# Loading a block's token rows in two transfers of 64 rows, each left out where it holds no row of the block

## The reference, cut to what matters

```
logits = x @ router_w.T + expert_bias
probs = sigmoid(logits); top_w, top_idx = top_k(probs, 8)
h1 = silu(einsum('th,eih->eti', x, w_gate))          # 256 -> 128 per expert
routed = einsum('eti,ehi->th', h1 * combine, w_down) # 128 -> 256, summed over 8 experts
x = layernorm(x + routed + shared)
```

## Time and profile before

| what | value |
|---|---|
| median of the three runs | 1122.46 us |
| profiled execution, its own time | 1123.29 us |
| its span, first to last instruction | 1121.5 us |
| mean granted TensorE clock | 0.951 |
| busy share of the span: TensorE, VectorE, ScalarE, GpSimd | 85%, 76%, 56%, 67% |
| DMA in the expert stage: busy share of the 16 engines | about 0.9 |

### The profile page before, as it was taken

How to read it: one execution, slowest core, us unless ns; L and a number is a source line. 1 busy time by engine, 2 the same in 40 slices (tenths; PEclk the granted TensorE clock), 3 DMA queues, 4 the chain that set the end, 5 groups by cost and what they waited for, 6 DMA issues and landing times. The chain is left out here.

```text
span 1121.5 us, 17555 instructions
## 1 busy us (share of the span) xinstructions
PE 957.9 (85%) x4878; PEld 801.3 (71%) x4878; DVE 848.6 (76%) x1645; ACT 625.9 (56%) x1555; POOL 746.0 (67%) x648
## 2 busy tenths in 40 slices
PE   6598989999999999999987989706989999899475
PEld 4476767888887887887866877605878778787354
DVE  0669999899999999999999994764656555555175
ACT  4766685875874865865864644403545555545100
POOL 1445576748679888888978986564777777777400
PEclk9698999999999999999988999957999999999699
DMA  7472854924124224134133012238998989997596
GB/s 237 169 253 77 252 171 151 300 71 162 45 63 143 76 68 153 62 100 133 40 126 118 37 48 75 101 120 260 326 301 262 297 281 287 285 294 244 187 377 222
DMA packets 118461, 195.48 MB, mean 174 GB/s; under 512 B 17684, under 2 KB 83378, under 8 KB 115922
## 3 DMA queue, kind: packets, MB, share of 16 engines
q1 hardware_dynamic: 79890, 134.54, 37.5%
q0 software_dynamic: 16512, 35.19, 8.6%
q10 hardware_dynamic: 21952, 24.51, 6.8%
HBM read 155.21 MB, written 75.64 MB: 206 GB/s over the span
## 5 line engine op out<-in xcount | busy, mean ns | idle before, releaser
L449 POOL TENSOR_TENSOR inf_all<-bc_all,du 128x1024 f32<-128x1024 f32 x128 | 300.6, 2365 | 102.3 <-DVEq L1647 62.0
L1649 DVE TENSOR_TENSOR_SCAN DA<-DA,inf_all 128x1024 f32<-128x1024 f32 x128 | 293.1, 2289 | 15.8 <-ACT DA L712 12.9
L1104 PE MATMUL Y<-hb_all,ident 128*128 128x256 f32 x1024 | 248.6, 391 | 21.9 <-DVE u L1665 21.6
L2196 POOL DMA_INDIRECT yp_dram<-u,sz x216 | 212.8, 985 | 78.9 <-issue 45.7
L1104 PEld LDWEIGHTS Y<-hb_all,ident 128*128 128x128 f32 x1024 | 197.6, 196 | 55.4 <-DVE u L1665 26.1
L712 ACT ACTIVATE DA<-dl,a_neg 128x255 f32<-128x255 f32 x512 | 211.9, 461 | 0.2
L2263 ACT ACTIVATE u<-DA,sz 128x256 f32<-128x256 f32 x216 | 102.3, 474 | 117.3 <-DMA yp_dram<-u,sz 83.7
L1656 DVE TENSOR_TENSOR hb_all<-DA,bc_all 128x1024 f32<-128x1024 f32 x128 | 156.0, 1219 | 7.9 <-DVE DA L1649 0.5
L2231 PE MATMUL DA<-hb_all,sz 128*128 128x256 f32 x432 | 136.5, 398 | 20.1 <-ACT sz L2256 19.0
L2224 PE MATMUL DA<-sz,hb_all 128*128 128x128 f32 x864 | 133.2, 277 | 3.8 <-issue 3.8
L2224 PEld LDWEIGHTS DA<-sz,hb_all 128*128 128x128 f32 x864 | 114.7, 193 | 4.2 <-issue 4.2
(11 more groups left out here) (453 smaller groups left out, 1599.9 us busy)
## 6 DMA issues: line engine op xcount, KB each, us to landing
hb_all<-in_w_moe SPq DMA_DIRECT2D x216, 256.0 KB
bc_all<-bc_dram SPq DMA_DIRECT2D x32, 1024.0 KB, 5.8
inf_all<-xe_dram SPq DMA_DIRECT2D x216, 140.0 KB
bc_all<-yp_dram SPq DMA_DIRECT2D x16, 1024.0 KB, 6.1
xe_dram<-zeros ACTq DMA_DIRECT2D x2, 7420.0 KB, 25.7
xe_dram<-zeros ACTq DMA_DIRECT2D x1, 7560.0 KB, 26.9
yp_dram<-u,sz POOLq DMA_INDIRECT x216
xt<-in_xT SPq DMA_DIRECT2D x8, 256.0 KB, 6.0
```

Of the source, the lines that this page charges most:

```text
L449: g.tensor_tensor(inf[(b * NTAU + t) % NI][:, :, :], bc[gr][:, 0, :, :], du[p][:, c, :].unsqueeze(1).to_broadcast([P, SG, T]), ALU.mult).t ...
L1104: ins = mm(Y[:, 0:T], ident[:, :], hb[t % NH][:, n, :], start=gr == 0 and n == 0, stop=gr == NG - 1 and n == SG - 1, skip_group_check=True)
L1649: v.tensor_tensor_scan(da[:, :], da[:, :], inf[(b * NTAU + t) % NI][:, :, :].rearrange("p n t -> p (n t)"), 0.0, ALU.mult, ALU.add).then_i ...
L2196: g.indirect_dma_start(yp_dram, bass.IndirectOffsetOnAxis(ap=pid[:, half * UNROLL + s_:half * UNROLL + s_ + 1], axis=0), ys[s_][:, :], Non ...
```

## The change

A block's rows are loaded by two transfers of 64 rows (`PARTS` = 2). The table has three values for a block (two row offsets and the weights' offset). VectorE adds a large number to the offset of a part in which no row belongs to the block, from turn 1 on; a transfer with such an offset is left out, as the weights' already are, and its semaphore still counts. In turn 0 both parts of all blocks are loaded. `ways` now takes the values of two blocks (6) in one load. Who waited for 16 on a slot's semaphore now waits for 32.

```diff
+SKIPPED = 1 << 19
+PARTS = 2
+PROWS = P // PARTS
+PWAY = PARTS + 1
...
-        xg_in = [sig(f"xg_in{i}", 16) for i in range(UNROLL)]
+        xg_in = [sig(f"xg_in{i}", 16 * PARTS) for i in range(UNROLL)]
...
-            def ways(i, h):
+            def ways(i, s_):
                 _, got = nc.values_load_multi_w_load_instructions(
-                    tabs[0:1, bass.ds((i * UNROLL + h * QUAD) * 2, QUAD * 2)], engines=[mybir.EngineType.SP],
+                    tabs[0:1, bass.ds((i * UNROLL + s_) * PWAY, PAIR * PWAY)], engines=[mybir.EngineType.SP],
...
-            def tokens(i, s_, r):
+            def tokens(i, s_, parts):
                 if gt_d.at(i - 1, s_ // PAIR + 1, True):
                     sp.wait_ge(gt_d.sem, gt_d.at(i - 1, s_ // PAIR + 1))
-                sp.dma_start(xg_i[s_].bitcast(U8), rows_at[bass.ds(r, P * X_BYTES)].rearrange("(p c) -> p c", p=P)).then_inc(xg_in[s_].sem, 16)
+                for f, r in enumerate(parts):
+                    sp.dma_start(xg_i[s_][f * PROWS:(f + 1) * PROWS, :].bitcast(U8),
+                                 rows_at[bass.ds(r, PROWS * X_BYTES)].rearrange("(p c) -> p c", p=PROWS),
+                                 bounds_check="skip_entire_dma").then_inc(xg_in[s_].sem, 16)
...
             def body(i):
-                for h in range(UNROLL // QUAD):
-                    got = ways(i, h)
-                    for q in range(QUAD):
-                        tokens(i, h * QUAD + q, got[q][0])
-                        weights(i, h * QUAD + q, got[q][1])
+                for lo in range(0, UNROLL, PAIR):
+                    for q, (parts, w) in enumerate(ways(i, lo)):
+                        tokens(i, lo + q, parts)
+                        weights(i, lo + q, w)
...
-                pe.wait_ge(xg_in[s_].sem, xg_in[s_].at(i, 16))
+                pe.wait_ge(xg_in[s_].sem, xg_in[s_].at(i, 16 * PARTS))
...
+            v.scalar_tensor_tensor(first_row[:, :], blk_b[:, :], float(P), blk_s[:, :], ALU.mult, ALU.subtract)
+            v.scalar_tensor_tensor(end_row[:, :], blk_q[:, :], float(P), blk_s[:, :], ALU.add, ALU.subtract)
+            v.tensor_scalar(later[:, :], turn_f[:, :], 0.0, None, ALU.is_gt)
...
-            v.tensor_scalar(way[:, :, 0], blk_h[:, :], float(X_BYTES), None, ALU.mult)
+            for f in range(PARTS):
+                v.tensor_scalar(missed[:, :, f], first_row[:, :], float((f + 1) * PROWS), None, ALU.is_ge)
+                ins = v.tensor_scalar(part_at[:, :, f], blk_h[:, :], float(f * PROWS), None, ALU.add)
+            link(ins)
+            for f in range(PARTS):
+                ins = v.scalar_tensor_tensor(missed[:, :, f], end_row[:, :], float(f * PROWS), missed[:, :, f], ALU.is_le, ALU.max)
+            link(ins)
+            link(v.scalar_tensor_tensor(missed[:, :, :], missed[:, :, :], float(SKIPPED),
+                                        later[:, :].unsqueeze(2).to_broadcast([BJ, 3, PARTS]), ALU.mult, ALU.mult))
+            link(v.tensor_tensor(part_at[:, :, :], part_at[:, :, :], missed[:, :, :], ALU.add))
+            v.tensor_scalar(way[:, :, 0:PARTS], part_at[:, :, :], float(X_BYTES), None, ALU.mult)
```

More of the change, by code:

```diff
@@ L98, in decoder_kernel @@
         blk_dram = nc.dram_tensor("blk_dram", (3, NBLK), I32, kind="Internal").ap()
-        way_dram = nc.dram_tensor("way_dram", (NBLK, 2), I32, kind="Internal").ap()
+        way_dram = nc.dram_tensor("way_dram", (NBLK, PWAY), I32, kind="Internal").ap()
         w_in = sb("w_in", [P, KD, 2 * DI])
@@ L2086, in decoder_kernel @@
         BASE = 19 * NE + 6 * NBLK
-        tabs = bc_flat[0:1, BASE:BASE + 2 * NBLK].bitcast(I32)
-        few = iter(range(BASE + 2 * NBLK, NG * 2 * SG * T, 16))
+        tabs = bc_flat[0:1, BASE:BASE + PWAY * NBLK].bitcast(I32)
+        few = iter(range(BASE + PWAY * NBLK, NG * 2 * SG * T, 16))
         def small(parts=BJ, width=3, dt=FP32):
@@ L2097, in decoder_kernel @@
         over, blk_j, blk_p, blk_w = (small() for _ in range(4))
-        way = small(BJ, 6, I32).rearrange("p (c f) -> p c f", f=2)
+        way = small(BJ, 3 * PWAY, I32).rearrange("p (c f) -> p c f", f=PWAY)
+        first_row, end_row, later = small(), small(), small()
+        missed, part_at = (small(BJ, 3 * PARTS).rearrange("p (c f) -> p c f", f=PARTS) for _ in range(2))
         blk_i = small(BJ, 9, I32).rearrange("p (f c) -> p f c", c=3)
@@ L2115, in decoder_kernel @@
         CN = PB[:, QT * NE:(QT + 1) * NE]
-        TAB_DONE = 23
+        TAB_DONE = 27
         def last_filled(eng):
@@ L2148, in experts_sync @@
             experts_at = a["w_moe"].rearrange("r c -> (r c)").bitcast(U8)
-            def ways(i, h):
+            def ways(i, s_):
                 _, got = nc.values_load_multi_w_load_instructions(
-                    tabs[0:1, bass.ds((i * UNROLL + h * QUAD) * 2, QUAD * 2)], engines=[mybir.EngineType.SP],
-                    min_val=0, max_val=(ROWS_X - P) * X_BYTES,
+                    tabs[0:1, bass.ds((i * UNROLL + s_) * PWAY, PAIR * PWAY)], engines=[mybir.EngineType.SP],
+                    min_val=0, max_val=2 * SKIPPED * X_BYTES,
                     skip_runtime_bounds_check_because="the table holds byte offsets of blocks' rows and of experts' weights")
[L2155 to L2158, removed]
-            def tokens(i, s_, r):
+                return [([nc.s_assert_within(got[q * PWAY + f], 0, (ROWS_X - PROWS) * X_BYTES,
+                                             skip_runtime_bounds_check_because="the copy is left out where a part holds no row of the block")
+                          for f in range(PARTS)],
+                         nc.s_assert_within(got[q * PWAY + PARTS], 0, (NE - 1) * W_BYTES,
+                                            skip_runtime_bounds_check_because="the copy is left out from NE on")) for q in range(PAIR)]
+            def tokens(i, s_, parts):
                 if gt_d.at(i - 1, s_ // PAIR + 1, True):
                     sp.wait_ge(gt_d.sem, gt_d.at(i - 1, s_ // PAIR + 1))
-                sp.dma_start(xg_i[s_].bitcast(U8), rows_at[bass.ds(r, P * X_BYTES)].rearrange("(p c) -> p c", p=P)).then_inc(xg_in[s_].sem, 16)
+                for f, r in enumerate(parts):
+                    sp.dma_start(xg_i[s_][f * PROWS:(f + 1) * PROWS, :].bitcast(U8),
+                                 rows_at[bass.ds(r, PROWS * X_BYTES)].rearrange("(p c) -> p c", p=PROWS),
+                                 bounds_check="skip_entire_dma").then_inc(xg_in[s_].sem, 16)
             def weights(i, s_, w):
@@ L2171, in body @@
             def body(i):
-                for h in range(UNROLL // QUAD):
-                    got = ways(i, h)
-                    for q in range(QUAD):
-                        tokens(i, h * QUAD + q, got[q][0])
-                        weights(i, h * QUAD + q, got[q][1])
-            for h in range(UNROLL // QUAD):
-                for q, (r, w) in enumerate(ways(0, h)):
-                    weights(0, h * QUAD + q, w)
+                for lo in range(0, UNROLL, PAIR):
+                    for q, (parts, w) in enumerate(ways(i, lo)):
+                        tokens(i, lo + q, parts)
+                        weights(i, lo + q, w)
+            for lo in range(0, UNROLL, PAIR):
+                for q, (parts, w) in enumerate(ways(0, lo)):
+                    weights(0, lo + q, w)
             sp.wait_ge(scat.sem, scat.at(NB - 1, 16 * QT * TOPK))
-            for h in range(UNROLL // QUAD):
-                for q, (r, w) in enumerate(ways(0, h)):
-                    tokens(0, h * QUAD + q, r)
+            for lo in range(0, UNROLL, PAIR):
+                for q, (parts, w) in enumerate(ways(0, lo)):
+                    tokens(0, lo + q, parts)
             further_turns(sp, last, body)
@@ L2346, in experts_vector @@
             v.tensor_copy(blk_i[:, 0, :], blk_e[:, :])
-            link(v.tensor_scalar(way[:, :, 1], blk_w[:, :], float(W_BYTES), None, ALU.mult))
+            link(v.tensor_scalar(way[:, :, PARTS], blk_w[:, :], float(W_BYTES), None, ALU.mult))
             assert steps[0] == TAB_DONE and UNROLL == 1 << 3 and P == 1 << 7
@@ L2368, in look_up @@
                 for s_ in range(lo, hi):
-                    dve.wait_ge(xg_in[s_].sem, xg_in[s_].at(i, 16))
+                    dve.wait_ge(xg_in[s_].sem, xg_in[s_].at(i, 16 * PARTS))
                 if dn_c.at(i - 1, hi, True):
```

## The result

The changed kernel takes 1282.26 us (median of four runs, 1278.79 to 1284.68), the one before 1123.71 in four runs beside them: a ratio of 1.141, 95% interval 1.137 to 1.146. Forecast were 1143 us, in a range of 1124 to 1153. The direction and the new bound were right, the size was not. The profiled execution of after took 1282.3 us, its span 1280.5.

The account below looks back on a forecast made before the run. GpSimd's scatters bound the kernel before (216 x 1.29 = 279 us). SyncE, with 289.6 us in turns 1 to 26, would become the bound and the last scatter come 20 us later: 1123.3 + 20 = 1143 us, range 1124 to 1153.

Parts of the forecast that it names:

- its terms: SyncE's work in turns 1 to 26: issues, skips, register loads and branches at their prices, 289.6 us in sum.
- so the price is per transfer: SyncE's token issues: 128 rows take 432 ns and 16 rows 430, so 64 rows cost all of 0.33 us.
- the ends lie close, and I keep 0.534: SyncE's register loads: one value takes 0.485 us, eight 0.534, so six values were put at 0.534.
- the start and the end of the stage: Token issues still start at 765.61, turn 1 at 774.7, SyncE ends at 1064.3; last scatter 20 us later.
- the cover that the prediction counted on: Before the first token issue, SyncE's 4.3 us wait for the front's last scatter hides 2.5 us of added work.
- TensorE's clock: In the stage: no fall expected, with TensorE's busy share going to about 85%.
- The first (GpSimd stays the bound): Rival: 64-row parts are cheaper for SyncE to issue than taken, so GpSimd stays the bound: 1124 us, chance 0.16.
- the second: Rival: SyncE stays below 1.29 us per block and lighter DMA load shortens GpSimd's scatters: 1119 us, chance 0.05.
- the third: Rival: skipping fails, or a skipped part costs SyncE as much as an issued one: 1171 us, chance 0.04.

Follow-up runs that it names:

- e8: The kernel before, from turn 1 on leaving out the first 128 words of each row, with no more instructions: 1120.72 us against 1120.15, ratio 1.000.
- e9: The changed kernel with its parts cut at row 48 instead of 64 (48 and 80 rows): 1216.65 us, ratio 1.083 to the kernel before.
- e3: The changed kernel with an unused fourth table value per block, so a register load takes 8 values: 1222.37 us, ratio 1.089 to the kernel before.
- e2: The changed kernel with both halves always loaded and no bounds check on them: 1330.14 us, ratio 1.185 to the kernel before.
- e11: The kernel before with other cuts in each slot, among them 64 rows in other widths and from other starts: 1275.26 us in a single run.

## Why the prediction was wrong in size

**What held.** GpSimd bound the stage before, and neither bytes nor the DMA share did (e8). The counts held: 321 parts issued, 95 left out, 112 and 96 for the weights, 104 loads. So did the mechanism: SyncE becomes the bound, its waits go (63.5 to 4.6 us), the scatters wait for data. Where the two dear prices are not paid, its terms come out within 3%: 235.9 us of issues and skips in e9 (forecast 229.1), and 61.2 of loads with their gaps in e3 (forecast 59.4).

**Where the difference lies.** The last scatter was forecast 20 us later than before and came 159.3 later. Of the 139.3 us between, 66 are issues and skips, 57 register loads, 5 waits and branches, 7 the start of turn 1 and 5 the way from SyncE's end to the last scatter.

**First failed step: "so the price is per transfer".** It rested on 128 and 16 rows, and all of 0.33 was taken because "those rows lie on both sides of 64". The price is per transfer for every size that was tried but one, and the change uses that one. A 64-row issue takes 0.47 to 0.55 instead of 0.33 to 0.38, the weight issue behind it 0.53 in the rows of after, and a part left out 0.14 instead of 0.08: +66 us. Removing only this (e9) gave back 66 of the 159 us.

**Second failed step: "the ends lie close, and I keep 0.534".** The ends were one value and eight. Eight are two aligned fours, six are not, and 0.485 isn't the price of one value in this stage (0.27). Six cost 0.72, or 1.27 and more, 1.08 on average: +57 us. Removing only this (e3) gave back 60. The Trainium skill, "DMA: Bandwidth & Descriptors", Latency and other measured facts, puts the floor of such a load at about 600 ns; the runs show less, 0.27 us for one value, 0.31 for four and 0.53 for eight.

**Third, small: the start and the end of the stage.** Turn 1 began at 781.5 where 774.7 were forecast. Of these 6.8 us 4.9 are turn 0, at the same two prices. The other 1.9 are the first token issue, at 767.54 instead of 765.61, and that is not shown to come from the change: the front's last scatter started 2.9 us later in this execution.

```profile
759.25 1.13 POOL L594 DMA_INDIRECT xe_dram<-th,sz  x1 [0.30 <-issue]
...
762.14 0.96 POOL L598 DMA_INDIRECT xe_dram<-th,sz  x1 [0.30 <-issue]
```

In e2, with the same loads, the first token issue came at 764.65. The loads ahead of the first weight issues did use up the cover that the prediction counted on: they took 0.9 to 1.7 us each, and SyncE's wait of 4.3 us for that scatter is gone. At the other end, the way from SyncE's end to the last scatter took 11.4 us, where 6.7 were forecast and 16.7 stood before.

TensorE's clock did fall, to a mean of 0.90 in a window with TensorE busy 68%, where 85% and no fall were forecast: from 880 to 884 us it was 1.00, the level of 2.4 GHz, with TensorE busy 2.60 us, and from 890 to 895 0.53, mostly the level of 1.2 GHz. TensorE sat idle for 166.7 us in all before its transposes until rows landed, so it is argued, not tested, that the clock set no end.

**The rivals.** The first (GpSimd stays the bound) needed a cheaper 64-row issue and fell with e2; the second with e8; the third with e2, though a skip at 0.14 was dearer than forecast. No run beat the kernel before, and nothing tried touches what bounds it, GpSimd's 216 scatters.

## What to carry to other kernels

An engine that only issues has a budget per block like any other: count its instructions and price each in the form in which the change will issue it. Two measured ends don't bound what lies between where the price has steps; a row of the very size, or a run of it alone, does. Lay out a table that is loaded into registers so that each load begins at a multiple of 16 B and takes whole fours, with an unused value if need be: that alone was worth 60 us here.

## What the runs showed of the hardware

A transfer of exactly 64 rows takes SyncE 0.47 us to issue, whatever its bytes (0.55 from row 32 on, and as the second part in the changed kernel), where transfers of 8 to 48 and of 80 to 128 rows took 0.29 to 0.41; an issue of another size behind it takes some 0.14 more (e11, and the weight issues of after). The times of register loads fit values taken by fours from a multiple of 16 B, else singly: 0.27 for one, 0.31 for four, 0.53 for eight, 0.98 for sixteen, 1.11 for five off the multiple. `skip_entire_dma` adds nothing to an issue (0.333 us with and without), and a transfer that it leaves out costs 0.08, in parts of 64 rows 0.14.
